# Perceiver block: last head pair of cross attention in token halves, with its projection, residual and norm begun tile by tile

## The chip, the cores and the metric

The kernel runs on one NeuronCore of one Trainium2 chip, as one launch of one program. Its engines work side by side and meet at semaphores: TensorE (PE) multiplies, VectorE (DVE), ScalarE (ACT) and GpSimd (POOL) do elementwise work, SyncE (SP) issues the transfers. The metric is the device time of a run in microseconds (us).

## What is computed

512 tokens of width 512 pass through three layers, each on a layer norm of the running `x` and added to it; all in fp32.

```python
x = x + _L0_xattn_ref(_layernorm(x), ctx, Wq, Wk, Wv, Wo, gq, gk)   # 16 heads of 128, 2048 context tokens
x = x + _L0_attn_ref(_layernorm(x), q_w, ..., o_w, o_b)             # linear attention in chunks of 64
x = x + _L0_ffn_ref(_layernorm(x), gate_w, w1, w2, w3, sw1, sw2, sw3)  # 32 experts, 6 per token, and a shared one

# cross attention
q, k = rmsnorm(q, gq), rmsnorm(k, gk)
attn = softmax(einsum('bqhd,bkhd->bhqk', q, k) * scale)
return einsum('bhqk,bkhd->bqhd', attn, v).reshape(B, Sq, H * D) @ Wo
# linear attention
attn = einsum('bnhid,bnhjd->bnhij', l2norm(q), l2norm(k))
out = einsum('bnhij,bnhjd->bnhid', attn * mask, softplus(hs @ b_w.T + b_b) * v)
return out * silu(hs @ og_w.T) @ o_w.T + o_b
```

## The kernel before

Tokens stand in 4 tiles of 128 (`TT = 4`), heads go in 8 pairs (`HP = 8`). A product of fp32 values is made of three matmuls (`mm3`, L314 to L318): each operand is split into a high part, which ACT rounds, and a low part, the difference, which DVE or POOL makes. So every operand passes ACT and then DVE or POOL before PE can use it, and most waits around the change are for these two parts. Products go into 8 banks of PSUM, `ps[:, bank, :]`, and a bank can be written again only when its reader is done. There is no scheduler: each engine's program is written out by hand in its own block, runs in that order, and waits on semaphores by count.

The start: SP loads key weights and the transposed context in four pieces of 512 columns each (L1079 to L1096), ACT and DVE split them, and PE computes all keys, 4 groups of 16 tiles (`keys`, L1714), of which ACT squares and DVE sums the squares. The first layer norm falls among them.

Cross attention, one pair of heads at a time: PE makes scores (`xa_pe_scores`, banks 4, 5, 0, 1), DVE and ACT the softmax, PE transposes the probabilities (`xa_pe_pT`, banks 6 and 7), multiplies them with the context (`xa_pe_u`, banks 4 and 5), and the result with the value weights (`xa_pe_ao`, banks 6 and 7). ACT and DVE split that in `xo_act_heads` and `xo_dve_heads`. The output projection of a pair, `xo_pe`, is done one pair later, in banks `YB = (2, 3, 6, 7)`, and `xo_dve` adds it to `x`. `pair(HP - 1, False, HP - 2)` is the last pair; after it stands `xo_pe(e, HP - 1)` with nothing beside it, then the whole second norm: `layernorm_dve`, 16 transposes in `layernorm_pe`, the high and low parts.

Linear attention, per pair (`la_pe`): projections K and Q (banks 0 to 3), their sums of squares, V in four token tiles (banks 4 and 5), the q k products (`at`), the gate G (banks 6 and 7), and the product with V. Ahead of the loop PE computes `beta`. ACT and POOL split the weights of each pair (`la_act_split`, `la_pool_split`); those of pair 0 come after cross attention. Behind the last pair follow the projection `wo_pe`, four adds (`add_y`), the third norm, the gate logits, and the experts. The shared expert comes first, as 8 steps of one token tile and half of its width (`ex_up`, `ex_down`, `NSH = 8`), with a step of the router behind the products of each (`router_steps`).

```python
            pair(HP - 1, False, HP - 2)
            xo_pe(e, HP - 1)
            e.wait_ge(y_ps, X1)
            e.sem_inc(wo_mm, H)
            layernorm_pe(e, 1, xn_b)
```

## Time and profile before

| | |
|---|---|
| median of 3 runs | 1038.76 us (1038.08 to 1039.44) |
| the profiled execution | 1036.27 us |
| its span, first to last instruction | 1034.5 us |
| PE busy | 988.1 us, 96% |
| DVE busy | 668.9 us, 65% |
| ACT busy | 541.1 us, 52% |
| POOL busy | 246.5 us, 24% |
| mean granted PE clock | 0.990 |

The profile is of one execution. Starts are us from the span's first instruction. The granted clock is a share of 2.4 GHz. A wait is put down to the instruction that released it, and "issue" is time in which an engine waited for nothing that the profile shows. The modelled ends of matmuls overlap, so the pace of matmuls is read from one start to the next.

### The profile page before, as it was taken

What the parts mean: (1) busy time and instruction counts of PE and PEld (TensorE: products, weight loads), DVE (VectorE), ACT (ScalarE), POOL (GpSimd) and SP (SyncE); (2) the same over time, 40 slices, a digit from 0 to 9 for tenths busy, and PEclk for the clock granted to TensorE, in tenths of its full rate; (3) what the DMA queues carried; (4) which work ended last, traced back from release to release, by engine and by line L of the source; (5) the groups of instructions that cost most, each with busy time, mean ns of one, the idle gap of its engine ahead of it and who ended that gap; (6) DMA issues with size and microseconds to landing.
All of it is one profiled execution on the core that took longest, in us unless ns stands there. A gap on an engine that the chain in (4) does not pass through costs nothing.

```text
span 1034.5 us, 18651 instructions
## 1 busy us (share of the span) xinstructions
PE 988.1 (96%) x5440; PEld 826.4 (80%) x5441; DVE 668.9 (65%) x1014; ACT 541.1 (52%) x885; POOL 246.5 (24%) x170
## 2 busy tenths in 40 slices
PE   6899899999999978999999999979999999999997
PEld 5788698989988866888888887757878777778784
DVE  5655655676557735778766675746656767667765
ACT  5544575666666545455455552541345555555551
POOL 1300221222122130333333300010023343333331
PEclk9999999999999999999999999989999999999999
DMA  9100353321232331222122105310567898998995
GB/s 322 34 0 1 84 197 103 101 77 39 87 101 60 74 107 46 81 81 81 61 81 81 41 21 189 103 41 1 209 212 232 289 317 280 346 329 287 291 329 153
DMA packets 75277, 144.00 MB, mean 139 GB/s; under 512 B 13444, under 2 KB 40452, under 8 KB 74992
## 3 DMA queue, kind: packets, MB, share of 16 engines
q1 hardware_dynamic: 67392, 131.48, 37.6%
q0 software_dynamic: 7856, 12.16, 5.5%
q8 instruction: 15, 0.25, 0.1%
q14 instruction: 14, 0.11, 0.0%
HBM read 146.86 MB, written 14.02 MB: 156 GB/s over the span
## 4 chain that ended last, share of the span: by engine, by line
PE 80%; DVE 6%; DMA 5%; ACT 3%; issue 3%; SPq 2%; DVEq 0%; ACTq 0%
PE ps L316 19%; PE ps L317 19%; PE ps L318 19%; PE ps L874 8%; PE ps L670 6%; DMA w_raw<-in_w 3%; PE ps L736 1%; PE ps L746 1%; PE ps L729 1%; DMA w_and_lists<-in_w 1%; PE ps L917 1%; DMA wo_raw<-in_owT 1%; SPq L845 1%; PE ps L863 1%; PE ps L349 1%
## 5 line engine op out<-in xcount | busy, mean ns | idle before, releaser
L888 DVE TENSOR_TENSOR w_l<-w_raw,w_h 128x1408 fp32r<-128x1408 f32 x76 | 121.5, 1623 | 30.3 <-ACT w_h L884 20.8
L884 ACT ACTIVATE w_h<-w_raw 128x1408 fp32r (+1 forms) x76 | 102.5, 1372 | 40.2 <-DMA w_raw<-in_w 28.9
L874 PE MATMUL ps<-w_and_lists,hT 128*128 (+3 forms) x264 | 121.3, 595 | 0.0
L692 POOL TENSOR_TENSOR lw_l<-lw_raw,lw_h 128x1024 fp32r<-128x1024 f32 x32 | 77.1, 2415 | 146.4 <-ACT lw_h L688 145.9
L316 PE MATMUL ps<-w_h,xeT_h 128*128 x288 | 96.8, 336 | 2.6 <-DVE w_l L888 2.1
L317 PE MATMUL ps<-w_l,xeT_h 128*128 x288 | 93.0, 323 | 0.0
L318 PE MATMUL ps<-w_h,xeT_l 128*128 x288 | 92.9, 323 | 0.0
L990 POOL DMA_INDIRECT xe<-xn_scratch,take x37 | 39.5, 1069 | 222.8 <-DVE ob L957 143.8
L874 PEld LDWEIGHTS ps<-w_and_lists,hT 128*128 128x128 f32 (+1 forms) x264 | 48.1, 189 | 43.7 <-issue 43.1
L316 PE MATMUL ps<-xT_hi,lw_h 128*128 128x512 f32 x192 | 77.3, 402 | 0.0
L317 PE MATMUL ps<-xT_lo,lw_h 128*128 128x512 f32 x192 | 76.4, 398 | 0.0
L318 PE MATMUL ps<-xT_hi,lw_l 128*128 128x512 f32 x192 | 75.5, 393 | 0.0
L1424 DVE TENSOR_REDUCE ssk<-sqk 128x4 f32<-128x512 f32 (+1 forms) x64 | 43.6, 685 | 38.5 <-ACT sqk L1302 38.2
L1302 ACT ACTIVATE sqk<-ps 128x512 f32<-128x512 f32 x64 | 38.2, 598 | 48.8 <-PE ps L318 43.8
L670 PE MATMUL ps<-pT,ctx 128*128 128x128 f32 x512 | 63.1, 280 | 0.3
L316 PE MATMUL ps<-wk_h,cT_h 128*128 128x512 f32 (+1 forms) x128 | 51.9, 405 | 11.2 <-DVE cT_l L1420 8.5
L670 PEld LDWEIGHTS ps<-pT,ctx 128*128 128x128 f32 x512 | 60.3, 195 | 1.7 <-ACT pT L542 1.7
L994 POOL DMA_INDIRECT y_scratch<-ob,give x34 | 55.3, 1626 | 20.9 <-DVE ob L957 11.1
L897 DVE TENSOR_TENSOR h<-h,ps 128x352 f32<-128x352 f32 x44 | 22.9, 521 | 57.5 <-PE ps L318 57.5
L552 POOL TENSOR_TENSOR wq_l<-wq_raw,wq_h 128x1024 fp32r<-128x1024 f32 x8 | 19.3, 2415 | 168.7 <-ACT wq_h L512 168.7
L316 PEld LDWEIGHTS ps<-w_h,xeT_h 128*128 128x128 f32 x288 | 54.4, 189 | 5.8 <-issue 5.8
L783 DVE RECIPROCAL q_r<-q_r 128x512 f32<-128x512 f32 x16 | 53.6, 3348 | 6.1 <-ACT q_r L759 6.1
(306 smaller groups left out, 2563.9 us busy)
## 6 DMA issues: line engine op xcount, KB each, us to landing
w_raw<-in_w SPq DMA_DIRECT2D x78, 704.0 KB
w_and_lists<-in_w SPq DMA_DIRECT2D x39, 512.0 KB
w_and_lists<-in_w SPq DMA_DIRECT2D x39, 192.0 KB
rkB<-rk_scratch SPq DMA_DIRECT2D x56, 128.0 KB, 3.2
wq_raw<-in_Wq SPq DMA_DIRECT2D x8, 512.0 KB, 4.8
wo_raw<-in_Wo SPq DMA_DIRECT2D x16, 256.0 KB, 2.8
lw_raw<-in_kwT SPq DMA_DIRECT2D x8, 512.0 KB, 3.4
lw_raw<-in_qwT SPq DMA_DIRECT2D x8, 512.0 KB, 3.3
```

What stands on the lines that cost most here:

```text
L316: nc.tensor.matmul(out_ap, lh, rh, start=first, stop=False)
L317: nc.tensor.matmul(out_ap, lh, rl, start=False, stop=False)
L318: return nc.tensor.matmul(out_ap, ll, rh, start=False, stop=last)
L670: m = e.matmul(ps[:, 4 + j % 2, at:at + P], ctx[:, b * KPB + t, hcol(c)], pT[:, b, t, :], start=t == 0, stop=t == KPB - 1)
L692: e.tensor_tensor(lw_l[n][:, :, :], lw_raw[n][:, :, :], lw_h[n][:, :, :], ALU.subtract).then_inc(lw_ready[n], 1)
L783: e.reciprocal(q_r[:, k, :], q_r[:, k, :]).then_inc(q_recip, 1)
L874: m = e.matmul(ps[:, 6 + k, :], hT[r, k, c, :], w2_raw[r, slot(w), c, :], start=c == 0, stop=c == FC - 1)
L884: e.activation(w13_h[:, k, n, :, :], w13_raw[:, slot(raw), n, :, :], ACT.Copy).then_inc(w13_hi_s, 1)
L888: e.tensor_tensor(w13_l[:, k, n, :, :], w13_raw[:, slot(raw), n, :, :], w13_h[:, k, n, :, :], ALU.subtract).then_inc(w13_ready, 1)
L990: e.indirect_dma_start(xe[:, k, :], None, xn_dram.ap(), bass.IndirectOffsetOnAxis(ap=take[:, k:k + 1], axis=0), bounds_check=T - 1, oob_is ...
L994: e.indirect_dma_start(y_dram[k].ap(), bass.IndirectOffsetOnAxis(ap=give[:, k:k + 1], axis=0), ob[:, k, :], None, bounds_check=T - 1, oob_ ...
L1424: e.tensor_reduce(ssk[:, t, bass.ds(g * 4, 4)], sqk[:, t % 2, :].rearrange("p (h n) -> p h n", n=P), AX.X, ALU.add).then_inc(sqk_free, 1)
```

## The change

Six edits are in it.

1. **First loads.** The context's first piece is 128 columns, its second 384; the first key weights come in two pieces, one for each half of the contraction. The context's first piece is issued ahead of the weights, and `x` behind the fourth context piece. PE runs 8 matmuls of constants before anything has landed.
2. **Last pair of cross attention.** It has code of its own, `last_pair`, on each engine. The projection of pair 6 goes into banks 2, 3, 0, 1 (`YL`). The product with the value weights is made for tokens 0 to 255 as soon as their `u` is split, and for the others later; `xo_pe_tile` projects tile 0 in between. The semaphore counts of `ao` grow by 2 (`AO = H + 2`).
3. **Second norm.** Each tile is added, measured, scaled, transposed and split by itself. The four transposed tiles go into banks 2, 3, 0, 1.
4. **Weights of linear pair 0.** ACT splits V, K and Q within the last cross pair, and POOL after its last weights there; G follows. `lw_h` and `lw_l` have other places in SBUF for that.
5. **First linear pair**, `la_pe_first`: V tiles 0 to 2 follow the transposes of their tiles, then beta, K, Q, V tile 3; half of G stands ahead of `at`, half behind it. DVE adds the output bias to `x` ahead of the softplus chain of beta. The other pairs keep their order.
6. **Third norm and router.** Tile 0 is normed alone; the first shared tile's products stand behind its transposes, the other tiles' transposes behind those, and the gate logits within the second shared tile.

The cut diff shows, in this order, the new tables, the last pair and the first linear pair on PE, the last pair on ACT, the weights on POOL, the matmuls on constants and the shared expert on PE.

```diff
+        LN_BANK = ((0, 1, 2, 3), (2, 3, 0, 1), (7, 6, 5, 4))
+        ctxT_parts = [slice(0, P), slice(P, G4)] + [slice(g * G4, (g + 1) * G4) for g in range(1, 4)]
+        wk_parts = [(slice(c, c + 1), slice(0, G4)) for c in range(CC)]\
+            + [(slice(0, CC), slice(g * G4, (g + 1) * G4)) for g in range(1, 4)]
+        YL = (2, 3, 0, 1)
...
+            def last_pair(i):
+                for j in range(JB):
+                    xa_pe_scores(e, i, j)
+                xo_pe(e, i - 1, last=True)
+                xa_pe_pT(e, i, 0)
+                xa_pe_pT(e, i, 1)
+                xa_pe_u(e, i, 0)
+                xa_pe_pT(e, i, 2)
+                xa_pe_u(e, i, 1)
+                xa_pe_pT(e, i, 3)
+                xa_pe_u(e, i, 2)
...
+                for k in range(2):
+                    xa_pe_ao_half(0, k).then_inc(ao_ps, 1)
+                xa_pe_u(e, i, 3)
...
+                xo_pe_tile(i, 0, YL[0])
+                e.wait_ge(u_ready, i * 4 + 4)
+                for k in range(2):
+                    xa_pe_ao_half(1, k).then_inc(ao_ps, 1)
+                xo_pe_tile(i, 1, YL[1])
+                e.wait_ge(ao_split, AO)
+                xo_pe_tile(i, 2, YL[2])
+                ln_tile_pe(e, 1, 0, xn_b)
+                xo_pe_tile(i, 3, YL[3])
...
+        def la_pe_first(e):
+            ln_tile_pe(e, 1, 1, xn_b)
...
+            la_pe_v(e, 0, 0)
+            ln_tile_pe(e, 1, 2, xn_b)
+            e.wait_ge(xT_ready, TT + 2)
+            la_pe_v(e, 0, 1)
+            ln_tile_pe(e, 1, 3, xn_b)
+            e.wait_ge(xT_ready, TT + 3)
+            la_pe_v(e, 0, 2)
...
+                xa_act_pT(e, i, 1)
+                xo_act_weights(e, i)
+                la_act_split(e, V_, 0)
+                xa_act_u(e, i, 0)
+                xa_act_pT(e, i, 2)
+                la_act_split(e, K_, 0)
+                xa_act_u(e, i, 1)
+                xa_act_pT(e, i, 3)
+                la_act_split(e, Q_, 0)
+                xa_act_u(e, i, 2)
+                xo_act_half(e, 0)
+                xa_act_u(e, i, 3)
+                e.activation(ln_std[:, TT:TT + 1], eps[:, :], ACT.Sqrt)
+                xo_act_half(e, 1)
...
             xo_pool_weights(e, HP - 1)
+            for n in (V_, K_, Q_):
+                la_pool_split(e, n, 0)
...
             e.tensor_tensor(bw_l[:, :, :], bw_raw[:, :, :], bw_h[:, :, :], ALU.subtract).then_inc(small_lo, 1)
-            for n in range(4):
-                la_pool_split(e, n, 0)
+            e.wait_ge(xn_ready, 2 * TT)
+            la_pool_split(e, G_, 0)
...
+            e.wait_ge(consts, 2)
+            for _ in range(8):
+                e.matmul(ps[:, 0, 0:P], ones[:, :], ones[:, :], start=True, stop=True)
...
+            ln_tile_pe(e, 2, 0, xn_c, strided)
+            e.wait_ge(x_ready, X2)
             for u in range(NSH):
...
+                ex_up_half(0, lh, ll, u % 2, w, 2 * w + 2)
+                if u == 1:
+                    gate_logits()
+                    ex_hT(e, 0, 0)
+                    logits()
+                ex_up_half(1, lh, ll, u % 2, w, 2 * w + 2)
+                if u == 0:
+                    for n in range(1, TT):
+                        ln_tile_pe(e, 2, n, xn_c, strided)
```

DVE at the end of cross attention, before: `u_l` and `ao_l` are the low parts of the attention's inner products, `x` the residual, `xT_lo` the low part of the normed tokens.

```order
L418 TENSOR_TENSOR x<-x,ps 128x512 x4
L606 TENSOR_TENSOR u_l<-ps,u_h 128x2x256 x4
L403 TENSOR_TENSOR ao_l<-ps,ao_h 128x512 x2
L418 TENSOR_TENSOR x<-x,ps 128x512 x4
L322 BN_STATS ln_stat<-x 128x6 x4
L328 BN_AGGR ln_mv<-ln_stat 128x2 x4
L332 RECIPROCAL ln_rstd<-ln_std 128x4
L336 TENSOR_SCALAR xn_b<-x,ln_mv,ln_rstd 128x512 x4
L372 TENSOR_TENSOR xT_lo<-ps,xT_hi 128x4x128 x4
```

The same place on DVE now, to the second tile's scale:

```order
L646 TENSOR_TENSOR u_l<-ps,u_h 128x2x256 x3
L449 TENSOR_TENSOR ao_l<-ps,ao_h 128x256 x2
L646 TENSOR_TENSOR u_l<-ps,u_h 128x2x256
L454 TENSOR_TENSOR x<-x,ps 128x512
L343 BN_STATS ln_stat<-x 128x6
L346 BN_AGGR ln_mv<-ln_stat 128x2
L449 TENSOR_TENSOR ao_l<-ps,ao_h 128x256 x2
L350 RECIPROCAL ln_rstd<-ln_std 128x1
L355 TENSOR_SCALAR xn_b<-x,ln_mv,ln_rstd 128x512
L454 TENSOR_TENSOR x<-x,ps 128x512
L343 BN_STATS ln_stat<-x 128x6
L346 BN_AGGR ln_mv<-ln_stat 128x2
```

The add and the statistics of tile 0 stand ahead of the second half of `ao_l`, and every tile's norm is a short chain of its own.

PE around the third norm, before: `gw` are the gate's weights, `w` the shared expert's.

```order
L349 MATMUL ps<-ident,xn_c 128x128 x16
L316 MATMUL ps<-xT_hi,gw_h 32x512
L317 MATMUL ps<-xT_lo,gw_h 32x512
L318 MATMUL ps<-xT_hi,gw_l 32x512
L316 MATMUL ps<-xT_hi,gw_h 32x512
```

And now, to the shared expert's first products:

```order
L320 MATMUL ps<-wo_h,ao_l 128x512
L363 MATMUL ps<-ident,xn_c 128x128 x4
L318 MATMUL ps<-w_h,xT_hi 128x352
L319 MATMUL ps<-w_l,xT_hi 128x352
L320 MATMUL ps<-w_h,xT_lo 128x352
```

4 transposes and 24 products of tile 0 stand where 16 transposes and the gate's products stood; the other 12 transposes follow them.

## Rows read from the trace of the kernel before

**Rows 1.** Waits of PE, whole span: whom for, us in total, times, longest.
```profile
PE ps L349 <- DVE xn_b L336: 5.2, 1, 5.2
PE ps L349 <- DVE xn_c L336: 4.8, 1, 4.8
PE ps L316 <- DVE xT_lo L372: 3.0, 2, 1.5
...
PE ps L657 <- DVE x L418: 2.2, 1, 2.2
```

**Rows 2.** Timeline of the start (start us, length us, engine, line, output<-inputs).
```profile
4.79 1.06 ACT L1297 ACTIVATE wk_h<-wk_raw 128x1024 fp32r<-128x1024 f32 x1 [2.38 <-DMA wk_raw<-in_Wk]
...
7.20 1.23 DVE L1420 TENSOR_TENSOR cT_l<-ctxT,cT_h 128x1024 fp32r<-128x1024 f32 x1
```

**Rows 3.** Chain that ended last (start us, us, what), first weight group.
```profile
8.53 0.76 PE ps L316
...
13.89 0.23 PE ps L316
...
32.73 0.24 PE ps L318
```

**Rows 4.** The same chain, end of cross attention and first pairs of linear.
```profile
361.13 1.68 PE ps L657 x8
...
388.93 3.56 PE ps L349 x16
...
393.99 0.39 PE ps L316
...
409.43 0.35 PE ps L706
...
425.29 1.78 PE ps L746 x16
...
454.21 1.78 PE ps L746 x16
```

**Rows 5.** Stretches: busy us (instructions) by engine, PEclk granted, DMA.
```profile
362.00:366.00 4.00, 4.00 (x24) 3.94 (x23) 0.00 (x0) 1.16 (x3) 0.16 (x1) 0.60 0.00 0
...
372.00:378.00 6.00, 3.04 (x13) 2.18 (x12) 2.08 (x3) 2.61 (x5) 0.00 (x0) 1.00 0.00 0
...
388.00:393.00 5.00, 3.55 (x16) 3.15 (x16) 4.32 (x7) 2.27 (x4) 0.60 (x1) 0.66 0.70 230
```

**Rows 6.** Timeline of DVE, second norm and first linear pair.
```profile
384.52 2.47 DVE L322 BATCH_NORM_STATS2 ln_stat<-x 128x6 f32<-128x512 f32 x4
...
393.15 0.69 DVE L372 TENSOR_TENSOR xT_lo<-ps,xT_hi 128x512 fp32r<-128x512 f32 x1 [0.16 <-ACT xT_hi L365]
...
412.77 3.35 DVE L783 RECIPROCAL q_r<-q_r 128x512 f32<-128x512 f32 x1 [0.76 <-ACT q_r L759]
...
416.59 2.08 DVE L802 TENSOR_SCALAR k_std<-k_std 128x8 f32<-128x8 f32 x1
...
423.44 1.28 DVE L816 TENSOR_TENSOR at<-ps,mask 128x512 f32<-128x512 f32 x2
```

**Rows 7.** Costly groups of the page: POOL's weight splits (count, busy, mean ns).
```profile
L692 POOL TENSOR_TENSOR lw_l<-lw_raw,lw_h 128x1024 fp32r<-128x1024 f32 x32 | 77.1, 2415 | 146.4 <-ACT lw_h L688 145.9
```

**Rows 8.** The chain again, from the projection's end into the experts.
```profile
673.15 2.74 DVE x L1494 x4
...
679.99 3.70 PE ps L349 x16
...
694.61 0.61 PE ps L863 x3
699.05 2.58 PE ps L874 x6
701.62 0.34 PE ps L863 x3
```

**Rows 9.** Stretch of the third norm and first shared tile.
```profile
676.00:702.00 26.00, 20.18 (x94) 15.33 (x95) 12.80 (x42) 11.18 (x23) 2.94 (x11) 0.80 0.11 41
```

More of the change, by code:

```diff
@@ new lines, in ln_tiles_inverse, with ln_tile_scale @@
+        def ln_tiles_inverse(e, first, last, std):
+            e.wait_ge(ln_std_ready, std)
+            e.reciprocal(ln_rstd[:, first:last], ln_std[:, first:last]).then_inc(dve_step, 1)
+            steps[0] += 1
+            e.wait_ge(dve_step, steps[0])
+        def ln_tile_scale(e, t, xn):
+            e.tensor_scalar(xn[:, t, :], x[:, t, :], ln_mv[:, t, 0:1], ln_rstd[:, t:t + 1],
+                            ALU.subtract, ALU.mult).then_inc(xn_ready, 1)
+        LN_BANK = ((0, 1, 2, 3), (2, 3, 0, 1), (7, 6, 5, 4))
@@ L368, in layernorm_split_dve, with ln_act_std @@
[L368 to L373 removed]
+            e.tensor_tensor(wk_l[:, c, kv], wk_raw[:, c, kv], wk_h[:, c, kv], ALU.subtract).then_inc(wk_ready, 1)
+        def ln_act_std(e, n, first, last):
+            e.wait_ge(ln_var_ready, TT * n + last)
+            e.activation(ln_std[:, first:last], ln_mv[:, first:last, 1], ACT.Sqrt, bias=eps[:, 0:1]).then_inc(ln_std_ready, 1)
@@ new lines, in la_pe_v, with la_pe_q_sum @@
+        def la_pe_v(e, i, t):
+            tk = slice(t * P, (t + 1) * P)
+            for c in range(DC):
+                m = mm3(ps[:, 4 + t // 2, (t % 2) * 2 * P:(t % 2 + 1) * 2 * P], xT_hi[:, c, tk], xT_lo[:, c, tk],
+                        lw_h[V_][:, c, :], lw_l[V_][:, c, :], c == 0, c == DC - 1)
+            if t % 2:
+                m.then_inc(v_ps, 1)
+        def la_pe_q_sum(e, i, k):
+            e.wait_ge(q_sq_split, i * 2 + (k + 1))
+            e.matmul(ps[:, 2 + k, :], ones_r[:, :], q_sqh[:, k, :], start=True, stop=False)
+            e.matmul(ps[:, 2 + k, :], ones_r[:, :], q_sql[:, k, :], start=False, stop=True).then_inc(q_ss_ps, 1)
@@ L732, in la_pe, with la_pe_k_sum, la_pe_at @@
+        def la_pe_k_sum(e):
+            for n in range(2):
+                for s in range(TT):
+                    m = e.matmul(ps[:, n, s * P:s * P + 1], kq_sq[:, n, s * P:(s + 1) * P], ones[:, 0:1],
+                                 start=True, stop=True)
+            m.then_inc(k_ss_ps, 1)
+        def la_pe_at(e, i):
             e.wait_ge(k_norm, i + 1)
@@ L1524, in _ @@
             step(e.scalar_tensor_tensor(beta[:, :, :].rearrange("p t h -> p (t h)"), sp[:, 0, :], 0.0, sp[:, 4, :], ALU.max, ALU.add))
-            e.wait_ge(lin_late, 32)
-            for t in range(TT):
-                e.tensor_tensor(x[:, t, :], x[:, t, :], ob_B[:, :], ALU.add).then_inc(dve_step, 1)
-            steps[0] += TT
-            e.wait_ge(dve_step, steps[0])
-            step(e.tensor_copy(ones_r[:, :], ones[:, :]))
             e.wait_ge(mask_ready, 1)
@@ L1722, in keys @@
                 for c in range(CC):
+                    if t == 0 and first:
+                        e.wait_ge(wk_ready, c + 1)
                     m = mm3(ps[:, 4 + t % 4, :], cT_h[:, c, tk], cT_l[:, c, tk],
```

433 lines of the change are left out of this document (271 added, 162 removed).

## The prediction, made before the changed kernel ran

> **What bounds the kernel now.** I first read which waits the tensor engine (PE) had, longest in total first [rows 1], because the chain that ended last is mostly PE: an edit is worth what it takes off PE's idle or slow time. The waits to see there are those of the layer norms (5.2 us before the second, 4.8 us before the third), of the residual adds (2.2 us) and three of 1.5 us, two of them behind a split into high and low parts. They lie in three places, so I then read each place: the start [rows 2, 3], the step from cross attention to linear attention [rows 4 to 7], and the step into the experts [rows 8, 9]. Between them the distance from one head pair's last product to the next one's is 454.21 - 425.29 = 28.9 us [rows 4], and PE has no idle time there worth naming; the change does not touch that code but for a wait on `sp_dve` that had long been met.
>
> **The start.** PE's first real matmul is at 8.53, behind the weight half landed at 4.79 and the low part of the context, done at 7.20 + 1.23 = 8.43 [rows 2]. Its first 12 matmuls take (13.89 - 8.53) / 12 = 0.45 us each, the other 84 of the first weight group (32.97 - 13.89) / 84 = 0.227 us: 1.2 GHz first, then 2.4 [rows 3]. The change loads 128 KB of context, then the weights in two pieces of 256 KB. By bytes the first weight piece lands some 0.5 us before the 512 KB did, at about 4.3; its high part takes half of 1.06 us, its low part half of 1.23 [rows 2], so the first matmul can start at about 5.6. The second piece lands where the old whole one did (0.64 MB in all against 0.5): about 5.1, split by 6.4. The second tile needs the other 384 columns, 0.4 MB later, about 6.2, then three quarters of 1.06 and of 1.23 us: 8.1. Before, it began at 8.53 + 6 x 0.45 = 11.2. From there 90 matmuls remain. At 2.4 GHz from the start they end at 8.1 + 20.4 = 28.5; if the clock rises only 5 us after 8.1, as it did 5 us after 8.53, 11 more are slow and they end at 31.0; if the first tile counts toward the rise, it comes near 10.5 and they end at 29.6. Before: 32.97. So 2.0 to 4.4 us, and I take **3.4**, since the first tile's work is continuous but for a moment. The 8 new matmuls on constants are 128 wide: at the pace of the 16 in 3.56 us [rows 4] they are over by about 3, well before 5.6. PE then idles some 2.6 us; a wait of 2.2 us is seen beside a granted clock of 0.60 in the stretch behind it [rows 1, 5]. I give them nothing. From the fifth tile on, context must be ready at 10.3, where it was; PE gets there at 12 or later. What is late next is what was late before: at 38 us PE waits for VectorE's (DVE) scaling of the first norm, whose own chain hangs on the last tile of the first group and so moves with it.
>
> **From cross to linear attention.** Before, PE has finished the projection of pair 6 at 358.9 and waits till 361.13 for the residual adds, since transposes share their banks [rows 1, 4]. The first 16 products and the transposes then run at a granted clock of 0.60 [rows 5]. Then come the 1.5 us waits, the 5.2 us wait for the whole norm, its 16 transposes at 0.66 (3.56 us where 2.4 GHz needs 1.7) and one more 1.5 us wait; the beta product begins at 393.99.
>
> After, the projection of pair 6 uses banks 2, 3, 0, 1, so the transposes follow at 358.8, and I pay 0.6 us for ScalarE's (ACT) copy. PE's work from there to beta at 2.4 GHz is 96 products and transposes of 128 columns at 1.78 / 16 = 0.111 us [rows 4] and 36 matmuls of 512 columns at 0.233: 19.1 us. The three V tiles moved ahead add 36 matmuls at half width, 3 x 1.4 = 4.2 us: 23.3. With no wait beta would start at 358.8 + 23.3 = 382.1. DVE does not allow that. Per tile it now has one add (0.69), statistics (0.62), aggregate, reciprocal and scale (about 0.9 with their hand-over) and one low part (0.69) [rows 6, 8], 2.9 to 3.2 us a tile, one after the other. The chain starts when the last `u` low part is done. Following the new order by hand with the durations of this trace, that is 370.7; two halves of `ao` in between cost 0.8; four tiles 4 x 3.2 = 12.8 and the last low part ends at 384.7. So beta starts at about 384.8 with three of four V tiles done: **9.2 us earlier**. ACT's three weight splits (1.05 us each) are now between its copies; they delay one `u` copy by 0.6 us, which is in the 370.7. POOL's splits of V, K and Q fill 363.6 to 370.9, all before PE asks for V at 378.5. The sqrt table's load is hidden behind PE's products.
>
> **Where part of that goes.** The 0.7 us wait for `betaT` also goes, being covered by K's first product, and copies that queue behind the beta chain cost PE about 0.4 before the first sum: the last Q product, which ended at 409.4 [rows 4], ends about 9.5 us earlier. What PE did early does not come out at the pair's end. DVE starts the 3.35 us reciprocal 3.4 us after that Q product, and 11.3 us later (412.77 to 424.1) the first masked product is ready [rows 6]; PE came to it at 425.29, so it was 1.0 us late. Now PE has 4.2 us less to do in between and waits: DVE's chain gives 9.5 + 1.0 = 10.5 us, and PE stands idle 2.5 us in front of it. That is as long as the 2.2 us wait that preceded a clock of 0.60, so 1.5 us of slow products come off: 9.0. **Term: 9.0**, from 10.5 (clock holds) down to 5 (the tile-by-tile stretch runs slow as well).
>
> The granted clock held at 1.00 through 372 to 378, where waits of 1.5 us stand around 3 us of products [rows 5]; the new stretch from 377 to 384 has three waits of 0.9 us or less with work between. By the row it holds. The Trainium skill (TensorE: Matmul & The Clock Gate, "HAM oscillation — how this bites in real kernels") speaks against this change: where each burst of products is shorter than the wait before the next, the array falls back to the low clock at every burst. By that rule V tiles 1 and 2 and the start of beta would run at half speed; that is the second rival below, priced from rows.
>
> **Into the experts.** Before: adds from 673.15, norm of four tiles, transposes at 679.99, a 1.5 us wait, gate logits, first shared tile, and the transposes that end tile 1 at 701.62 [rows 8]; the stretch has a granted clock of 0.80 [rows 9]. After, tile 0 is added, normed and transposed alone: 673.15 + 0.69 (add) + 0.9 (statistics, aggregate) + 0.7 (second add) + 0.2 + 0.54 (scale) puts PE's 4 transposes at 676.3 and its low part at 678.5. The first shared tile (24 matmuls, 694.94 to 699.05, about 4.0 us [rows 8]) runs 678.5 to 682.5 while DVE does the other three tiles' norm, in order: statistics to 681.1, scales to 683.3. The second tile's low part is ready at 684.2; 2.0 us of products; gate logits 2.8 us; the transposes of `h` and the logits; 2.0 us more; down product 2.6; transposes 0.5. With small waits of 0.4 for ACT's copy of the logits that ends at 695.6, against 701.96: 6.3 us. But PE idles 1.1 and 1.5 us with 0.4 us of work between, then starts slow: that puts 24 matmuls and what follows back by up to 1.7 us. I take **4.8**, between 4.3 and 6.3. The router's steps stay on the same tiles; DVE reaches PE's third tile with the list of choices just in time (before: 1.8 us to spare), and what comes later hangs on nothing that has a fixed time.
>
> **Sum.** 3.4 + 9.0 + 4.8 = 17.2 us. The profiled execution took 1036.27 us (span 1034.5): it would become 1019.1. The median of the runs is 2.5 us above that execution, so 1038.76 - 17.2 = **1021.6 us**.
>
> **The rivals.**
> Second, the low clock: the bursts fall to 1.2 GHz. In the middle two V tiles (2.8 us), 8 transposes (0.9) and half of beta (1.4) double, less the waits they fill: 9.0 - 3.5 = 5.5; at the experts the low end, 4.3, and at the start 2.0. Sum 11.8, time 1027. For it: 0.60 and 0.66 behind single waits; against: 1.00 at 372 to 378 [rows 5].
> Third, everything holds: 4.4 + 10.5 + 6.3 = 21.2 and perhaps a microsecond more, where a shift against the clock also saves the 1.5 us of slow matmuls after the wait at 38 us. Time 1016.5.
> Fourth, the early start does not reach the end: DVE's chain in the first pair gets longer. GpSimd (POOL) now splits K, Q and V of the next pair back to back while DVE handles V. One DVE instruction on 8 columns took 2.08 us where its neighbours take 0.2, while POOL's 2.42 us splits ran [rows 6, 7]. Two more such stops are 4.8 us: 17.2 - 4.8 = 12.4, and with the low clock 7. Time 1026.4 to 1032. The Trainium skill (SBUF — State Buffer, "SBUF: two separate sides") says of this pair that whichever starts first holds the shared port for its whole instruction; the row agrees.
> Fifth, slower: the clock falls at 377 and does not come back while waits keep recurring through the first pair. PE's work from 377 to 417 is about 33 us at 2.4 GHz, and doubles. It decides from some 19 us of work at half speed; the whole of it would give 33 - 17.2 = 16 us slower, 1055. Against it: after each fall in [rows 3, 5] it was back within 5 us of steady work, and beta, K and Q are 14 us of it.
>
> **How the numbers follow.** Forecast 50%, low clock 20%, everything holds 15%, longer chain 12%, slower 3%. The forecast case alone reaches from 1019 to 1025. Adding the low clock, everything-holds and the nearer end of the longer chain gives **1015 to 1029**, which leaves out the far end of the fourth, the fifth and a little of each side. What a measurement of this kernel can tell from no change is about 0.2%, 2.1 us. Faster by more: 0.94; within: 0.02; slower: 0.04.
>
> **What the changed profile would show.** PE's first product on real data at 5 to 6.5 us, and the first weight group over at 29 to 30. No wait behind the residual adds of pair 6; the beta product at 384 minus the start's gain; a new PE wait of about 2.5 us in front of the first pair's last products, for the masked product. The third norm's wait of 4.8 us replaced by two short ones, and the first shared tile under way before the gate logits. Pairs still 28.9 us apart. The prediction would be wrong if the pairs were longer, if stretches between 377 and 386 showed half clock, or if the new wait in the first pair were over 5 us.

## The result, and the profile after

| | before | after |
|---|---|---|
| median of 5 runs each, on one chip | 1038.66 us (1035.85 to 1039.44) | 1021.01 us (1018.99 to 1024.46) |
| ratio, 95% interval | | 0.9837 [0.9813, 0.9862] |
| the same kernel measured again, 6 runs | 1035.47 us | 1018.09 us, 0.9849 [0.9817, 0.9881] |

The change makes the kernel 15.6 us (by the second ratio) to 17 us (by the first) faster; 1021.6 us was predicted. Two profiled executions of the changed kernel exist. One, of 1024.46 us (span 1022.7, mean granted clock 0.993), is the slowest of its five runs; the other, of 1018.28 us (span 1016.5, clock 0.996), lies near the median of its six. Rows below are of the second unless they say otherwise; it is called the second profile.

The waits of TensorE (PE) in the second profile, longest in total first; columns as in [rows 1]:

```profile
PE ps L318 <- DVE ssk L1564: 2.6, 1, 2.6
PE ps L318 <- DVE w_l L992: 2.0, 4, 0.7
PE ps L787 <- DVE at L916: 1.9, 1, 1.9
PE ps L318 <- DVE wk_l L374: 1.8, 2, 1.3
PE ps L318 <- DVE ao_l L493: 1.8, 1, 1.8
...
PE ps L318 <- issue: 1.5, 1, 1.5
...
PE ps L363 <- DVE xn_b L355: 1.1, 2, 0.7
PE ps L363 <- DVE xn_c L355: 0.9, 1, 0.9
```

Against [rows 1]: the layer norms' 5.2 and 4.8 us are 1.1 and 0.9, and the 2.2 us behind the residual adds are gone. Gone from the middle are also one of the two 1.5 us waits for `xT_lo` and these two of the kernel before:

```profile
PE ps L316 <- DVE u_l L606: 1.5, 1, 1.5
PE ps L316 <- DVE ao_l L403: 1.5, 1, 1.5
```

New is 1.9 us in front of the first linear pair's last product (`at`, L916), where 2.5 was forecast. The wait for `ssk` at 38 us is as long as it was.

Where the 18 us between the two spans arose is read from the start of the same PE instruction in each trace. Times are us from the span's start; the last column is how far the second profile is ahead of before:

| PE reaches | before | second profile | first profile | ahead |
|---|---|---|---|---|
| first product on loaded data | 8.53 | 6.11 | 6.64 | 2.4 |
| end of the wait for `ssk` | 41.04 | 38.86 | 38.74 | 2.2 |
| first `u` product of pair 6 (L710) | 333.90 | 331.52 | 332.85 | 2.4 |
| `beta` | 393.99 | 382.76 | 384.06 | 11.2 |
| last products of the first linear pair (L787) | 425.13 | 411.92 | 414.29 | 13.2 |
| same of the second pair | 454.05 | 440.87 | 443.15 | 13.2 |
| last matmul of `wo_pe` | 674.77 | 662.05 | 663.79 | 12.7 |
| transposes of `h`, third shared tile | 708.9 | 690.2 | 692.0 | 18.7 |
| first transposes of gathered tokens (L1021) | 749.62 | 730.93 | 732.69 | 18.7 |
| the last ones | 1003.77 | 985.09 | 991.61 | 18.7 |

Between these two executions the start gives 2.2 to 2.4 us, the middle 10.8, the step into the experts 6; 0.5 us is given back in `wo_pe`, most of it in the wait for `ao_l` (1.8 us instead of 1.4), and 0.7 behind the last expert. The first linear pairs are 28.95 us apart (440.87 - 411.92), as before.

One pair of executions is a small sample, so here are the same stretches in all 14 profiles of this document, those of the experiments below included:

| stretch of PE | without the edit | with it |
|---|---|---|
| start to first `u` product of pair 6, with the 2.6 us wait for `ssk` | 333.90, 335.18 | 329.18 to 332.85 in 8 profiles (one of them without the constants), mean 331.0 |
| the same in kernels without that wait | 328.60 | 326.44, 326.85, 327.03 |
| from there to the first pair's last products (L787) | 91.2 to 91.5 in 3 profiles | 80.3 to 80.4 in 5 whose middle is that of the change, 81.4 in the first profile |
| last matmul of `wo_pe` to the third shared tile's transposes | 31.9 to 34.1 in 5 profiles, mean 32.9 | 28.1 or 28.2 in 5, 29.7 in 4, mean 28.8 |

The middle is nearly the same every time. At the start and at the third norm the gain differs by several us between executions, 3.5 and 4.0 us by the means.

The granted clock, by stretches of the two profiles, PE only. Columns: stretch, its length, PE busy and instructions, granted clock, DMA share, GB/s. The second profile:

```profile
362.00:366.00 4.00, 4.00 (x38) 1.00 0.00 0
...
372.00:378.00 6.00, 5.29 (x32) 1.00 0.85 235
378.00:384.00 6.00, 5.51 (x39) 1.00 1.04 357
384.00:396.00 12.00, 12.00 (x55) 1.00 0.10 33
...
404.00:410.00 6.00, 6.00 (x35) 1.00 0.55 175
```

and the first profile:

```profile
404.00:410.00 6.00, 6.00 (x17) 0.50 0.44 143
```

Full clock from 362 through 396 in both, where [rows 5] had 0.60 and 0.66 beside waits. The tile-by-tile stretch did not fall. The half clock at 404 to 410 in the first profile stands behind a wait of 0.5 us (for `q_sql`) that the second profile has too, without the fall.

### The profile page after: what moved, and what is told of

Its sections match the earlier page's. It is cut to its first block, busy times and chain, and to the rows that moved or that the text cites. A ratio compares the mean times of both kernels' runs of the same rounds, so it can differ in the third digit from the quotient of the medians.

```text
span 1022.7 us, 18723 instructions
## 1 busy us (share of the span) xinstructions
PE 993.1 (97%) x5468; PEld 828.9 (81%) x5469; DVE 669.1 (65%) x1022; ACT 541.0 (53%) x894; POOL 246.4 (24%) x170
## 4 chain that ended last, share of the span: by engine, by line
PE 74%; SPq 6%; DMA 6%; DVE 6%; issue 5%; ACT 4%; DVEq 0%; ACTq 0%
PE ps L318 19%; PE ps L319 18%; PE ps L320 18%; PE ps L710 6%; PE ps L978 6%; DMA w_raw<-in_w 4%; SPq L945 2%; PE ps L777 1%; PE ps L787 1%; SPq L1119 1%; PE ps L767 1%; DMA wo_raw<-in_owT 1%; DVE w_l L992 1%; ACT wo_h L406 1%; PE ps L697 1%
## 5 line engine op out<-in xcount | busy, mean ns | idle before, releaser
L318 PE MATMUL ps<-xT_hi,lw_h 128*128 128x512 f32 x192 | 78.3, 408 | 0.0
L710 PE MATMUL ps<-pT,ctx 128*128 128x128 f32 x512 | 62.1, 277 | 0.6 <-ACT pT L582 0.3
L710 PEld LDWEIGHTS ps<-pT,ctx 128*128 128x128 f32 x512 | 59.1, 192 | 2.2 <-ACT pT L582 2.2
L1098 POOL DMA_INDIRECT y_scratch<-ob,give x34 | 55.5, 1631 | 21.4 <-DVE ob L1061 11.6
L319 PEld LDWEIGHTS ps<-w_l,xeT_h 128*128 128x128 f32 x288 | 54.2, 188 | 0.0
```

Source lines behind the costliest of these rows:

```text
L318: nc.tensor.matmul(out_ap, lh, rh, start=first, stop=False)
L319: nc.tensor.matmul(out_ap, lh, rl, start=False, stop=False)
L710: m = e.matmul(ps[:, 4 + j % 2, at:at + P], ctx[:, b * KPB + t, hcol(c)], pT[:, b, t, :], start=t == 0, stop=t == KPB - 1)
L1098: e.indirect_dma_start(y_dram[k].ap(), bass.IndirectOffsetOnAxis(ap=give[:, k:k + 1], axis=0), ob[:, k, :], None, bounds_check=T - 1, oob_ ...
```

## The experiments

Each was measured beside the kernel before on the same chip; ratios are to it, so the bracketed intervals are what is compared between chips. Where two intervals overlap, a difference in us between them is an estimate, and the traces have to decide. First the change taken apart.

**The whole change again.** No edit.

> The changed kernel again, unedited, for a second profile and more runs. The profile of the changed kernel was of its slowest run (1024.5 us, granted clock 0.993): the experts took 258.9 us from the first to the last gather's transposes against 254.2 before, and the gate product of the first linear pair ran at 1.2 GHz. Theory A (chance): both are the state of that one execution; this profile shows the experts at about 254 us and the third shared tile about 17 us earlier than before. Theory B (caused): the experts take 258 to 259 us again, because the change makes them longer. By A the time is 1019 to 1021, by B 1021 to 1024.

1018.09 us, 0.9849 [0.9817, 0.9881]. Theory A held: the experts take 254.2 us, and the third shared tile comes 18.7 us earlier than before. This is the reference for all that follow.

**The start alone.** The kernel before, with the load pieces and the matmuls on constants of the change.

```diff
+        wk_parts = [(slice(c, c + 1), slice(0, G4)) for c in range(CC)]\
+            + [(slice(0, CC), slice(g * G4, (g + 1) * G4)) for g in range(1, 4)]
...
+            for _ in range(8):
+                e.matmul(ps[:, 0, 0:P], ones[:, :], ones[:, :], start=True, stop=True)
```

> The kernel before with only the smaller first loads and the 8 matmuls on constants. The predicted term was 3.4 us. The trace of the change shows the first real product 1.9 us earlier, the wait at 38 us 2.3 us earlier, and by the last cross pair only 1.0 to 1.1, since PE ran slow for longer behind that wait. Theory A: the slow stretch behind the wait is as long as the state of the clock makes it in a given run, so the mean gain is 2 us, 1036.5. Theory B: it is always longer, gain 1 us or none, 1037.7 or more.

1033.65 us, 0.9988 [0.9965, 1.0010]: 1.2 us faster, between 3.6 faster and 1 slower, so the run times do not resolve the gain. (In 4 of the 12 runs 3.0 to 3.3 us of the time lie outside the span, 1.7 to 2.1 in the others; the mean spans differ by 1.8 us.) Its trace is ahead of before by 3.2 us when the wait for `ssk` ends (37.86), by 4.7 at `u` of pair 6 (329.18) and by 3.9 at the end of its span. The difference between the first two is the clock: behind that wait it stayed at 1.00 here, and was low in the kernel before. Of the ten profiles with this wait it stayed at 1.00 in three, and was low for 3 to 7 us in seven. That is theory A's mechanism; the times do not tell it from theory B.

**The middle alone.** The change without the loads, the constants and the edit at the third norm.

```diff
-        wk_parts = [(slice(c, c + 1), slice(0, G4)) for c in range(CC)]\
...
-            for _ in range(8):
-                e.matmul(ps[:, 0, 0:P], ones[:, :], ones[:, :], start=True, stop=True)
...
-            ln_tile_pe(e, 2, 0, xn_c, strided)
-            e.wait_ge(x_ready, X2)
```

> The change without its first loads, its matmuls on constants and its third norm and router: only the last cross pair in halves, the second norm by tiles, the weights' splits and the first linear pair are left. The predicted term was 9.0 us, from 10.5 down to 5; the trace of the change gives 9.8 from the last scores to the end of the first linear pair. So 1029 us against 1038.7. A rival, in which the gain of 17 us comes mainly from the ends of the kernel and the middle is given back by the masked product's chain, gives 1034 or more.

1024.84 us, 0.9907 [0.9877, 0.9936]: 9.6 us, between 6.6 and 12.7, against a term of 9.0. The rival is excluded. In its trace PE goes from `u` of pair 6 to the first pair's last products in 80.35 us (335.18 to 415.53), before in 91.2.

**The third norm undone.** The change with only that edit taken back.

```diff
-            ln_tile_pe(e, 2, 0, xn_c, strided)
-            e.wait_ge(x_ready, X2)
...
+            for t in range(TT):
+                ln_tile_pe(e, 2, t, xn_c, strided)
```

> The change with its third norm and router as they were: all four tiles normed together, the gate product ahead of the first shared tile. The predicted term was 4.8 us, between 4.3 and 6.3, and the trace shows 6.15 between the end of the output projection and the third shared tile. So 6 us slower than the change, 1026 to 1027. A rival, in which the experts take back what they start earlier, gives at most 2 us of difference, 1021 to 1023.

1020.94 us, 0.9884 [0.9848, 0.9921]; the whole change has 0.9849, so the edit is worth 3.6 us by the ratios and 2.9 by the medians, where 6 were expected. The intervals overlap, so the times alone exclude neither nothing nor 6 us. From the last `wo_pe` matmul to the third shared tile's transposes PE takes 32.1 us (659.68 to 691.8) against 28.15 with the edit, 4.0 us. The kernel before took 34.1 for it. Both have the 4.8 us wait, and both run at half clock behind it, but not equally long. This kernel:

```profile
PE ps L363 <- DVE xn_c L355: 4.8, 1, 4.8
665.00:668.00 3.00, 3.00 (x15) 0.50 0.28 108
668.00:672.00 4.00, 2.50 (x12) 0.87 0.50 185
672.00:680.00 8.00, 7.68 (x49) 1.00 0.00 1
```

and the kernel before, where the wait ends at 679.99:

```profile
680.00:684.00 4.00, 3.68 (x16) 0.50 0.44 167
684.00:688.00 4.00, 2.82 (x7) 0.50 0.26 95
688.00:692.00 4.00, 4.00 (x19) 0.81 0.00 0
692.00:700.00 8.00, 7.68 (x47) 1.00 0.00 1
```

Behind the wait it was low for some 4 us here and 9.5 us there. That is 5.5 us more at half pace, worth 2.7 us, which accounts for the 2.

**The constants left out.**

```diff
-            e.wait_ge(consts, 2)
-            for _ in range(8):
-                e.matmul(ps[:, 0, 0:P], ones[:, :], ones[:, :], start=True, stop=True)
```

> The change without the 8 matmuls on constants. The prediction gave them nothing: no difference beyond 0.2%, and as many slow matmuls at the start, 8 to 13. A rival, in which they wake the clock, has 5 or more additional slow matmuls here, 1 us or more of loss.

1016.25 us, 0.9828 [0.9799, 0.9857], against 0.9849 [0.9817, 0.9881] with them: no gain from them. Without them the first products start 0.43 to 0.57 us apart, 1.2 GHz; there are 11 slow starts, 2 or 3 more than in the two profiles of the change, where the rival had 5 or more. With them they did so too in the first profile; in the second the first three are 0.23 to 0.31 us apart and the next ones slow again. Of the ten profiles with the constants, five begin fast and five slow, after idle times of 1.3 to 1.8 us and of 1.2 to 1.7. (Here the pace must be read from the starts: the clock column reads 1.00 from 6 to 9 us in the first profile, with starts 0.43 us apart.) Without them, then with them in the second profile:

```profile
6.66 0.77 PE L318 MATMUL ps<-wk_h,cT_h 128*128 128x512 f32 x1 [6.66 <-DVE wk_l L374]
7.23 0.63 PE L319 MATMUL ps<-wk_l,cT_h 128*128 128x512 f32 x1
```

```profile
6.11 0.47 PE L318 MATMUL ps<-wk_h,cT_h 128*128 128x512 f32 x1 [1.32 <-DVE wk_l L374]
6.42 0.39 PE L319 MATMUL ps<-wk_l,cT_h 128*128 128x512 f32 x1
```

The few tenths go into the wait for the next weight piece: the wait for `ssk` ends at 38.97 without and at 38.86 with them.

**The weight splits put back.** ACT's V, K and Q splits and POOL's stand behind cross attention, as before, and POOL does not wait for the norm's scaling there; the rest is the change.

```diff
-            for n in (V_, K_, Q_):
-                la_pool_split(e, n, 0)
...
-            e.wait_ge(xn_ready, 2 * TT)
-            la_pool_split(e, G_, 0)
+            for n in (V_, K_, Q_, G_):
+                la_pool_split(e, n, 0)
...
-                la_act_split(e, V_, 0)
...
-                la_act_split(e, K_, 0)
...
-                la_act_split(e, Q_, 0)
...
-            la_act_split(e, G_, 0)
+            for n in (V_, K_, Q_, G_):
+                la_act_split(e, n, 0)
```

> The change with the weight splits of V, K and Q of linear pair 0 back behind cross attention, on ACT ahead of G's and on POOL without the wait for the norm. The prediction named them as cover that costs nothing inside the last pair. Here ACT's three splits (3.1 us) stand ahead of the second tile's high part and POOL's overlap DVE's scales, so V tile 0 can start only some 2.5 us later and the beta product 2 to 4 us later; at the first pair's end 2 to 3 us of it should be left, since DVE's chain there moves with PE. Rival: 0.5 us or less is left, the splits were no part of the gain.

1022.05 us, 0.9877 [0.9858, 0.9895], 2.9 us worse than the change by the two ratios, whose intervals overlap. The trace shows the cover going: PE comes to V of tile 0 before POOL has its low part, waits 2.5 us, and from 380.0 to 383.2 its products of 256 columns start 0.21 us apart instead of 0.12.

```profile
378.99 0.39 PE L318 MATMUL ps<-lw_h,xT_hi 128*128 128x256 f32 x1 [2.46 <-POOL lw_l L739]
```

PE comes from `u` of the last pair to `beta` in 28.3 us instead of 25.1, and from `u` of pair 6 to the first pair's last products in 83.6 instead of 80.4: 3.2 us, where 2 to 3 were expected and the rival had 0.5 or less. The missing cover may not be all of it: beside POOL's splits two of DVE's scalings of `xn_b` take 1.18 and 1.16 us instead of 0.55, a kind of stop that the next experiments are about.

**What holds the first linear pair now?** The prediction put the new wait (1.9 us here) at the end of VectorE's (DVE) chain: Q's 3.35 us reciprocal first, then V. So the reciprocal was moved behind everything PE waits for.

```diff
             q_split(1)
-            q_inverse(0)
             for g in range(2):
...
+            q_inverse(0)
             q_inverse(1)
```

> The change with one order turned in every linear pair: DVE takes the 3.35 us reciprocal of the first head's query norm behind the masked products instead of ahead of the V copies. If DVE's chain in the first pair is what the early V tiles run into (PE waits 1.9 us for the masked product there in the second profile of the change), the first masked product is ready 3.35 us earlier and that wait is gone: 1.9 us faster than the change, the other pairs as they were (28.9 us). A rival: that wait has another source (the two DVE instructions of 2.0 us that stand behind POOL's splits); then they move forward with the rest and at least 1 us of the wait stays. A loss would mean that the gate behind the masked products becomes late.

1020.02 us, 0.9858 [0.9826, 0.9890], not told apart from the change. My theory fell and the rival held: with 3.35 us taken out of the way, PE still waited 1.7 us for `at`. DVE's rows tell why. Columns: start, length, engine, line, operation, count, and in brackets the idle time before and who ended it. First the change (second profile), then this kernel:

```profile
400.80 3.35 DVE L883 RECIPROCAL q_r<-q_r 128x512 f32<-128x512 f32 x1 [0.76 <-ACT q_r L859]
404.07 0.63 DVE L897 TENSOR_TENSOR vt<-ps,v_bias 128x512 f32<-128x512 f32 x1
404.61 1.99 DVE L902 TENSOR_SCALAR k_std<-k_std 128x8 f32<-128x8 f32 x1
...
406.97 2.01 DVE L906 TENSOR_TENSOR v_scale<-k_r,beta 128x8 f32<-128x8 f32 x1
409.02 0.76 DVE L912 TENSOR_TENSOR vt<-vt,v_scale 128x256 f32<-128x256 f32 x2
...
411.09 1.28 DVE L916 TENSOR_TENSOR at<-ps,mask 128x512 f32<-128x512 f32 x2
```

```profile
402.67 1.47 DVE L901 TENSOR_SCALAR k_std<-k_std 128x8 f32<-128x8 f32 x1 [2.11 <-ACT k_std L863]
...
406.54 2.94 DVE L911 TENSOR_TENSOR vt<-vt,v_scale 128x256 f32<-128x256 f32 x2
```

POOL's rows of the change at that time:

```profile
401.79 7.17 POOL L739 TENSOR_TENSOR lw_l<-lw_raw,lw_h 128x1024 fp32r<-128x1024 f32 x3 [19.59 <-ACT lw_h L735]
```

Three weight splits of POOL run back to back, 401.79 to 408.96, and so end near 404.2, 406.6 and 409.0. In the change `k_std` and `v_scale` end with the second and the third of them (406.60, 408.98), although they have 8 columns; the reciprocal beside the first takes its usual 3.35 us. With the reciprocal moved, `k_std` is caught by the first split, `v_scale` (1.76 us) by the second and the scaling of V by the third. Moving DVE's work within that stretch changes which instructions are caught, not when the chain gets out. In [rows 6] the same held: `k_std` took 2.08 us, and the two scalings of V behind it 2.88:

```profile
419.24 2.88 DVE L812 TENSOR_TENSOR vt<-vt,v_scale 128x256 f32<-128x256 f32 x2
```

**POOL behind V.** So the next kernel moves POOL instead: it does not start on the next pair's splits until DVE has scaled V.

```diff
             with e.Fori(0, HP - 1) as i:
+                e.wait_ge(v_ready, i * 2 + 2)
                 for n in range(4):
                     la_pool_split(e, n, i + 1)
```

> The change with one wait more: in each linear pair POOL splits the next pair's weights only when DVE has scaled V. With the late reciprocal the PE wait for the masked product stayed (1.7 us for 1.9), and DVE's small instructions on 8 columns ended with POOL's splits each time. If POOL's splits hold DVE up, these instructions take 0.2 us here, the masked product is ready 3 us or more earlier, and the 1.9 us wait of PE in the first pair is gone: up to 1.9 us faster than the change, the other pairs at 28.9 us as before. The rival: POOL, now later, is late with K for the next pair, and every one of the 7 pairs loses; at 0.5 us each that is 3.5 us slower.

1017.33 us, 0.9812 [0.9787, 0.9837]. DVE's rows:

```profile
399.19 3.35 DVE L883 RECIPROCAL q_r<-q_r 128x512 f32<-128x512 f32 x1 [0.76 <-ACT q_r L859]
...
403.00 0.16 DVE L902 TENSOR_SCALAR k_std<-k_std 128x8 f32<-128x8 f32 x1
...
403.53 0.17 DVE L906 TENSOR_TENSOR v_scale<-k_r,beta 128x8 f32<-128x8 f32 x1
403.74 0.76 DVE L912 TENSOR_TENSOR vt<-vt,v_scale 128x256 f32<-128x256 f32 x2
...
405.81 1.28 DVE L916 TENSOR_TENSOR at<-ps,mask 128x512 f32<-128x512 f32 x2
```

The two small instructions take 0.16 and 0.17 us, the chain from reciprocal to `at` 7.9 us instead of 11.6, and PE no longer waits for `at`: it gets from `u` of pair 6 to that product in 78.3 us instead of 80.4. The trace settles the mechanism; the times alone (0.9812 and 0.9849, intervals that overlap) do not. In each of the 12 profiles without this wait one or two of these small instructions take 1.4 to 2.1 us in the first pair, and at least one takes about 2 us in every further pair but the last; in the two profiles with it none does in any pair. The rival did not occur: the next pairs are 28.9 us apart here too. Nor did they gain, so the same stop costs nothing in the later pairs. The 3.7 us off DVE bring 2.1, since PE is then the later of the two.

**POOL behind the scaling at 33 us.** The wait for `ssk` at 38 us was read as the end of DVE's chain through the first norm. In it four scalings of 512 columns took 4.93 us beside POOL's first two splits of weights:

```profile
33.28 4.93 DVE L338 TENSOR_SCALAR xn_a<-x,ln_mv,ln_rstd 128x512 f32<-128x512 f32 x4
...
34.06 2.46 POOL L592 TENSOR_TENSOR wq_l<-wq_raw,wq_h 128x1024 fp32r<-128x1024 f32 x1 [6.02 <-ACT wq_h L552]
36.49 1.44 POOL L594 TENSOR_TENSOR wkT_l<-wkT_raw,wkT_h 128x512 fp32r<-128x512 f32 x1
```

The first two scalings, begun ahead of POOL, take 0.55 and 0.54 us, the third and fourth 2.61 and 1.48.

```diff
+            e.wait_ge(xn_ready, TT)
             xa_pool_weights(e, 0)
```

> The change with one wait more: POOL begins to split the first query weights only when DVE has scaled the first norm. In every profile PE waits 2.6 us at 38 us, before and after the change, and DVE's four scales take 4.9 us there against 1.9 to 2.3 in the other norms. If POOL's split holds a port that DVE's scale needs, the scales take 2.2 us here, the wait of PE goes, and with it the slow products behind it: 2.6 to 4.5 us faster than the change. If the scales are long for another reason, nothing changes.

1014.65 us, 0.9816 [0.9787, 0.9844], 3.4 us less than the change by the ratios, with intervals that overlap. The trace decides again. The scalings take 1.92 us and PE has no wait there at all:

```profile
33.10 1.92 DVE L338 TENSOR_SCALAR xn_a<-x,ln_mv,ln_rstd 128x512 f32<-128x512 f32 x4
...
35.10 2.41 POOL L592 TENSOR_TENSOR wq_l<-wq_raw,wq_h 128x1024 fp32r<-128x1024 f32 x1 [7.21 <-DVE xn_a L338]
```

When PE begins the first pair the kernel is 4.5 us ahead of the second profile (127.41 against 131.95 at the first `u` product): the 2.6 us wait, and some 1.6 us of slow matmuls behind it (seven starts 0.42 to 0.59 us apart in the second profile, 0.23 from then on). The second part is not certain in every execution, since the clock does not always fall behind that wait.

**The same wait in the kernel before,** and nothing else of the change, to see whether the gain needs the change:

> The kernel before with nothing but the POOL wait behind the first norm's scale. The same wait of 2.6 us stood there, with slow products behind it. If it is a matter of the port alone and not of the change, PE's wait at 38 to 41 us is gone here too, and the kernel is 2.6 to 4.5 us faster than before, ratio 0.996 to 0.9975.

1030.40 us, 0.9958 [0.9944, 0.9972]: 4.3 us faster than the kernel before, and here the interval excludes no gain. So the gain does not need the change; the kernel before had the same stop.

**Late reciprocal and POOL behind the scaling.** The edits of two kernels above together.

> The change with both edits, the late reciprocal and POOL behind the first scale. They lie in different places, so their gains add: 4.5 to 6.4 us faster than the change, 1012 to 1015 where the change is at 1018 to 1021. If the later stages give back what comes early, less.

1015.93 us, 0.9829 [0.9798, 0.9861], 2.1 us less than the change by the ratios where 4.5 to 6.4 were expected, and no better than without the late reciprocal (0.9816). Its gain does not show here either. PE no longer waits for `at` in this trace, but the clock was low for over 3 us behind the 0.5 us wait for `q_sql`, and PE was late by that.

**Both waits of POOL.**

> The change with both POOL waits, the one behind the first norm's scale (4.5 us at the second weight group's end by its trace) and the one behind the scaled V. Gains should add: 6 us faster than the change, and the fastest of all, 0.979 of the kernel before. If the second wait costs the later pairs more than it gives, slower than the kernel with the first wait alone (0.9816).

1012.99 us, 0.9794 [0.9780, 0.9807], 5.7 us less than the change where 6 were expected. It has the lowest ratio of all, and its interval lies below both intervals of the change; those of the kernels with one of the two waits overlap it, so the second wait's part is shown by the traces alone. Its profile (span 1008.4) shows a low clock behind the 0.5 us wait for `q_sql`, so the first linear pair gained only 0.6 us in it (79.8 us from `u` of pair 6 to the last products):

```profile
398.00:404.00 6.00, 6.00 (x29) 0.72 0.01 1
```

## Why the prediction was right, step by step

The time was right, 1021.6 against 1021.01: 17.2 us were forecast, and 17.6 is the difference of the medians (15.6 by the second measurement's ratio). That it is right to 0.6 us is luck: the first ratio's interval alone reaches from 14.3 to 19.4 us, and runs of the changed kernel lie 5 us apart. What is borne out is the mechanism, that the waits in three places go, and the size of the largest term. Not every step was right:

**The start: 3.4 forecast; 2.2 to 2.4 in the second profile, 3.5 on the mean of the profiles; the landings were mis-sized.** ScalarE (ACT) is released by each landing:

```profile
4.61 0.63 ACT L1404 ACTIVATE wk_h<-wk_raw 128x512 fp32r<-128x512 f32 x1 [1.15 <-DMA wk_raw<-in_Wk]
6.11 0.63 ACT L1404 ACTIVATE wk_h<-wk_raw 128x512 fp32r<-128x512 f32 x1 [0.87 <-DMA wk_raw<-in_Wk]
7.17 0.85 ACT L1399 ACTIVATE cT_h<-ctxT 128x768 fp32r<-128x768 f32 x1 [0.42 <-DMA ctxT<-in_ctxT_in]
```

Forecast were landings at 4.3, 5.1 and 6.2, by bytes. The first half of the weights is 256 KB, and is there hardly sooner than the whole 512 KB were ([rows 2]: 4.79); the second comes 1.5 us behind it and the context's 384 columns 1.1 us behind that. So the first product ran at 6.11 instead of 5.6 and the second tile could begin at 9.0 instead of 8.1, and the first weight group was over at 30.6, not at 29 to 30. The eleven profiles with these loads are alike: landings at 4.6 to 5.2, 5.9 to 6.6 and 7.1 to 7.7, first product at 6.1 to 6.7. The kernel before varies too, though. Its loads gave a first product at 8.53, 8.68 and 9.43 in three profiles, so one late landing does not make the whole term too large. Without the wait for `ssk`, where the clock stays at 1.00 to pair 6, the start is worth 1.6 to 2.2 us; with it the slow stretch behind that wait, 0 to 7 us long, decides what is seen. The constants are worth nothing, as forecast, but not for the reason given: they end at 4.7 to 5.0, not at 3, and PE idles 1.2 to 1.8 us behind them, not 2.6. In the end-to-end time the start is the weakest part: 1.2 us alone (not resolved), and by subtraction 2.4 us from the ratios (6.0 for start and third norm together, less 3.6) or 3.9 from the medians (6.8 less 2.9).

**The middle: 9.0 forecast, 10.8 in the profile, 9.6 in the time.** The steps held: `beta` was to come 9.2 us earlier and came 8.8 earlier, the start's gain taken out. The last low part was to end at 384.7, which is 382.3 less the start's real 2.4; it ended at 381.92 + 0.69 = 382.6. (The prediction's own figures, 370.7 + 0.8 + 12.8, make 384.3, not 384.7; the 0.4 is in none of its rows.) The step to it was partly another: DVE had scaled tile 3 at 379.72 already, but PE came to its transposes only at 380.65, behind V of tile 1. At the last tile PE's own work is the bound, not DVE's chain. The new wait is there, 1.9 us instead of 2.5 (9.5 + 4.2 - 10.5 of the prediction makes 3.2). The 1.5 us that were taken off for slow products behind it were not lost: the granted clock is 1.00 behind it in all seven profiles that have this wait (1.7 to 1.9 us). The gain therefore lies at the upper bound, 10.5. That the first profile shows 9.8 us here with a stretch at half clock is no contradiction: PE was late by the slow products, and did not have to wait for `at` afterwards (no wait for it in that trace). Slow clock and wait covered each other. Of the middle's edits only the weight splits were taken out by themselves (3.2 us of it in the trace); how the rest divides between the halves, the banks, the norm by tiles and the early V tiles is not shown.

**Third norm: 4.8 forecast; 3.6 in the time, 4.0 and 6 between profiles.** The order of events is as forecast: transposes of tile 0 behind 0.9 us, the first shared tile, the other twelve transposes, the second tile.

```profile
663.35 0.74 PE L363 MATMUL ps<-ident,xn_c 128*128 128x128 f32 x4 [0.91 <-DVE xn_c L355]
665.55 0.40 PE L318 MATMUL ps<-w_h,xT_hi 128*128 128x352 f32 x1 [1.46 <-issue]
...
669.47 1.59 PE L363 MATMUL ps<-ident,xn_c 128*128 128x128 f32 x12
671.51 0.43 PE L318 MATMUL ps<-w_h,xT_hi 128*128 128x352 f32 x1 [0.45 <-DVE xT_lo L388]
```

The granted clock is 1.00 from 664 to 694 here, although PE had idled twice. But the 1.7 us that I took off for this did come in other executions: in four of the nine profiles with this edit the clock falls in the first shared tile, and the step to the third tile takes 29.7 us instead of 28.1, 1.5 us more. This is one of them, the kernel with the late reciprocal:

```profile
666.83 0.49 PE L318 MATMUL ps<-w_h,xT_hi 128*128 128x352 f32 x1
667.12 0.50 PE L319 MATMUL ps<-w_l,xT_hi 128*128 128x352 f32 x1
```

Its starts are 0.29 us apart, where the second profile has 0.16. Of the 6 us between the profiles 2 come from how long the clock stayed low in the profile before [rows 9]; against the undone edit, whose clock was low for 4 us behind the wait, the gain is 4.0, and 4.0 is also the difference of the means. What was mis-sized in the 4.8 is the side before the change: the sum took its low clock from one profile, where it was one of the two longest of five.

**The rival of the low clock did not occur.** I had read the rule of the Trainium skill (TensorE: Matmul & The Clock Gate, "HAM oscillation — how this bites in real kernels") so that the bursts of V tiles 1 and 2 would run at half speed. Its condition is that a burst is shorter than the wait beside it, and that held neither in the forecast (waits of 0.9 us or less, bursts of 1.4 us and their transposes) nor in the run, so the run does not test the rule: the burst of a V tile, about 2.1 us with its transposes, follows waits of 0.7 and 0.4 us, and the granted clock was 1.00 in all of it. With the splits put back, behind a wait of 2.5 us there, it did fall.

**The rival of the longer DVE chain was half right, and I had its sign in the wrong place.** The locks are there, 1.99 and 2.01 us on instructions that take 0.16. But the kernel before had about as much: 2.08 on `k_std` and 2.88 on two scalings of V that take 0.76 (beyond their own time 4.0 us before, 3.7 after). It is not a loss that the change brings; it was one that stood there, and taking it away at both places was worth 5.7 us by the ratios, more than the start or the third norm. The Trainium skill (SBUF — State Buffer, "SBUF: two separate sides") names what excludes each other for a whole instruction: DVE with two SBUF inputs against a GpSimd instruction that reads SBUF, or DVE in a mode that uses both its ports against a GpSimd instruction. That `k_std` and the norm's scaling, which have one tensor input, were in such a mode is not shown by any row. The rows agree in what is stopped (`k_std`, `v_scale`, `vt<-vt`, the norm's scaling) and in what is not (the reciprocal at 400.80 and `vt<-ps,v_bias` at 404.07, both beside POOL's splits). I read one such row and priced the danger of more (4.8 us, two more stops); I did not look for what the existing ones cost.

**What moved behind.** The 18.7 us stand unchanged from 690 us to the last expert in the second profile; in the first, 4.7 us are lost between the first and the last expert (258.9 us against 254.2), in which PE's waits for `w_l` are 4.6 us instead of 2.0. The other profiles, whose experts are the same, took 252.6 to 257.0 us. Why the weights of the experts come later in one run is open; the change does not touch them. With the clock of single stretches it may be why runs of one kernel differ by 5 us.

## What to carry to other kernels

When an instruction on one engine is long at one place and short elsewhere, find its partner before planning around it: two waits on POOL, one line each, brought the kernel from 0.9849 to 0.9794, a third of what six edits had. Hold the engine that has time to spare (POOL is busy 24%) until the one on the chain is through. And where a layer norm stands between two stages, begin the next stage by tiles; the bound is then its own chain on DVE, some 3 us a tile, or PE's work between the tiles, and both can be added up beforehand. Last, read a term that hangs on the clock from several executions: what the low stretch behind one wait costs differed by up to 3 us between them.

## What the runs showed of the hardware that was not expected

- Small DVE instructions are not small beside POOL: 8 columns took 1.99, 2.01 and 2.08 us where they take 0.16 alone, and with the late reciprocal three POOL splits of 2.4 us in a row caught one DVE instruction each. In the later pairs the same stop cost nothing: they are 28.9 us apart with it and without.
- A smaller first load did not land much sooner: 256 KB were there at 4.61 behind 128 KB of context, 512 KB at 4.79 in the kernel before. Cut in two, the load brought its first half 0.2 us sooner, and its second 1.3 us later than the whole had come.
- Matmuls on constants until 5 us were followed by first products at full pace (0.3 us to the second start) in five of ten profiles and at half pace (0.6) in five; either way no gain in time was measured.
- The same wait in the same code is followed by a low clock in some runs and not in others: behind 0.5 us at 402 (low in three profiles, the first of the change and the two with POOL behind the scaling and a second edit; 1.00 in the eight others with this wait), behind 2.6 us at 38 us, low in seven profiles and 1.00 in three; and behind the 4.8 us before the third norm's transposes, low for 3 to 4 us in three profiles and 9.5 us in two. A price for a slow clock read from one profile is one draw.
